# Moving layer 2's mask from the scores to the sigmoids, on GpSimd, in a four-layer graph network with new instruction orders

## The chip, the cores and the metric

One NeuronCore of one Trainium2 chip runs the whole program. The metric is the device time of one execution in microseconds (us). The engines are TensorE (PE, with its weight loads as PEld), VectorE (DVE), ScalarE (ACT), GpSimd (POOL) and SyncE (SP), which issues nearly all the transfers. Each engine runs its own list of instructions in order; they meet only at semaphores.

## What is computed

Thirty-two graphs of 256 nodes with 128 features each go through four layers. Each adds its result to its input and normalises the sum:

```
x = layernorm(x + L0(x, adj))   # graph attention: softmax over neighbours of leaky(s_i + d_j), times h
x = layernorm(x + L1(x, adj))   # the same with other weights
x = layernorm(x + L2(x, adj))   # sigmoid(leaky((x*a0) @ x.T)) where adj == 1, and 0 where adj == 0; times x
x = layernorm(x + L3(x, adj))   # sum over neighbours, times a 128x128 weight, plus bias
```

Only layer 2 matters here. `adj` holds 0 and 1. An entry with `adj == 0` must have weight 0, and an entry with `adj == 1` has weight sigmoid(leaky(score)), where leaky(s) is the larger of s and 0.2 s. Since sigmoid rises everywhere, this is the larger of sigmoid(s) and sigmoid(0.2 s).

## The kernel before

The graphs go through in 16 teams of two (`H = 2`); a step named `score:5` does its work for both graphs of team 5. Every engine has a string of such steps in the table `ORDER` (written out by hand or by a tool, and fixed), and the program emits the instructions in exactly that order. There is no scheduler at run time: an engine whose next step waits for a semaphore stands still, with everything behind it. `BANKS` gives the PSUM bank (of 8) for every product of every team; PE waits for the last reader of a bank before it writes there. Rings of buffers in SBUF (`RAW`, `MASK`, `SG`, `WGT`, `XB` and so on teams deep) set how far apart the teams may be.

What happens to one team, with the engine that does it before the change:

- PE projects (`h0`), DVE takes the two attention logits (`logits0`), PE and DVE find their maximum (`dT0`, `peak0`, `top0`, `dmax0`), DVE subtracts it (`shift0`), ACT takes exponentials (`gains0`) and scales the values (`vals0`). PE spreads a row (`rows0`), DVE makes the masked weights (`weight0`, four instructions of 128x256), PE multiplies them with the values (`out0`), DVE divides by the row sums and adds the input (`rsum0`, `rinv0`, `res0`), and takes the statistics (`stats0`, `var0`). POOL raises the variance to the power -1/2 (`pow0`). Layer 1 repeats this with `1` in the names; `center1` and `norm1` end it.
- Layer 2: PE transposes (`xT2`), ACT copies with a factor (`xTa`), PE forms the scores (`score`). In the same accumulation PE adds a second product for each block: the tile `raw`, which is 1 - adj, times `minus_big`, -1e30 on the diagonal. A score without an edge so becomes -1e30, and both sigmoids of it are 0. ACT takes sigmoid(s) into `sg` and sigmoid(0.2 s) into `wgt` (step `sigmoid`), DVE writes the larger into `wgt` (step `alpha`), and PE multiplies (`out2`). DVE adds `xb`, which is x plus bias from POOL (`bias2`), and takes statistics (`res2`, `stats2`, `var2`); `pow2` is on POOL, and `norm2` on ACT or DVE.
- Layer 3: the normalised x is split into two half-precision parts (`high` on ACT, `low` on POOL), PE gathers over the mask (`agg`), ACT copies, PE multiplies (`out3`), DVE does `res3`, `stats3`, `var3`, POOL `pow3`, ACT or DVE `norm3`; SP stores.

From each adjacency tile (int32) two 16-bit tiles are made: `raw` by DVE (`make_raw`) and the mask `maskT` by ACT (`make_mask`). DVE also ORs each team's `raw` into `seen` (`note_seen`), and `judge` tests at the end whether any entry was other than 0 or 1; then a general path would run, which never happens for these inputs.

The lines that the prediction names are L731 `make_raw`, L738 `note_seen`, L754 and L538 the biases on DVE and POOL, L765 `norm` on DVE, L791 `shift`, L797 `fscale`, L815 `alpha`, L841 `res2` and `res3`, L856 statistics, L862 to L869 the variances, L873 `center1`, L542 the powers and L547 `low` on POOL, L571 `make_mask` and L637 `norm1` on ACT, L1089 and L1090 the two products of a score.

## Time and profile before

| what | value |
|---|---|
| device time, three runs | 270.17, 268.92, 270.03 us; median 270.03 |
| profiled execution, first to last instruction (span) | 268.6 us |
| instructions | 6069 |
| DVE busy | 247.2 us (92%) |
| PE busy | 237.0 us (88%) |
| ACT busy | 217.9 us (81%) |
| POOL busy | 139.0 us (52%) |
| DMA, share of 16 engines' span | under 24% in all queues |
| granted TensorE clock, mean | 0.978 of full |

The profile gives its execution's span and no other time of its own: 268.6 us lies 1.4 us under the median of the timed runs. "Busy" is time in which at least one instruction of the engine is open; a short instruction on DVE overlaps its follower by some 0.07 us, so a group's busy time is a little under its count times its mean. PE's busy time counts the latency of each product and not only its pitch.

### The profile page before, as it was taken

To read this page: it belongs to the slowest core of one execution; us is meant where nothing else is said; L and a number is where in the kernel's file an instruction comes from. 1 tells how busy PE (TensorE), PEld (TensorE's weight loads), DVE (VectorE), ACT (ScalarE), POOL (GpSimd) and SP (SyncE) were. 2 spreads that over 40 slices of the span, in tenths; PEclk is the share of its full clock that TensorE was granted. 3 is DMA by queue.
4 is the path that set the end of the run, shared out by engine and by line. 5 is a ranking of instruction groups with operands and counts; after the bars stand their busy time and mean duration, and the time that the engine had idled before them with its cause. 6 is when DMAs were issued, how large, how long until landed. Compare 5 with 4: busy or idle time off the path is not lost.

```text
span 268.6 us, 6069 instructions
## 1 busy us (share of the span) xinstructions
PE 237.0 (88%) x1825; PEld 210.1 (78%) x1825; DVE 247.2 (92%) x956; ACT 217.9 (81%) x626; POOL 139.0 (52%) x161
## 2 busy tenths in 40 slices
PE   7887969889998999999999899999999959996850
PEld 7765768678886989888898788988999859785740
DVE  1598998999999989999999999999999999999883
ACT  1366525688899999899899999999999979977841
POOL 1001102511384485689647717554598457778851
PEclk9999988999999999999999999999999999999985
DMA  6597371000070003506000633103000110100033
GB/s 237 193 307 264 118 248 67 1 2 0 2 263 13 2 0 115 202 14 221 1 5 0 198 114 122 41 1 121 0 2 0 41 41 7 36 0 1 4 117 122
DMA packets 12147, 21.79 MB, mean 81 GB/s; under 512 B 1104, under 2 KB 5968, under 8 KB 12112
## 3 DMA queue, kind: packets, MB, share of 16 engines
q1 hardware_dynamic: 11680, 21.17, 22.9%
q8 instruction: 16, 0.26, 0.4%
q10 hardware_dynamic: 432, 0.20, 0.3%
q14 instruction: 19, 0.16, 0.2%
HBM read 17.17 MB, written 4.19 MB: 80 GB/s over the span
## 4 chain that ended last, share of the span: by engine, by line
DVE 49%; PE 28%; issue 8%; POOL 6%; ACT 5%; DMA 2%; DVEq 0%; POOLq 0%; ACTq 0%
PE banks L1123 13%; DVE wgt_all L808 10%; DVE fstats L856 8%; DVE fres L849 7%; DVE fres L841 5%; POOL frstd L542 4%; DVE wgt_all L815 3%; PE banks L1089 3%; DVE raw_all L731 3%; PE banks L1064 2%; PE banks L1120 2%; PE banks L1133 2%; DMA adj_all<-adj_turned 2%; PE banks L1081 1%; PE banks L1049 1%
## 5 line engine op out<-in xcount | busy, mean ns | idle before, releaser
L542 POOL TENSOR_TENSOR frstd<-fvar,minus_half 128x4 f32<-128x4 f32 x64 | 74.2, 1165 | 104.7 <-DVE fvar L862 36.6
L1123 PE MATMUL banks<-vals_all,wgt_all 128*128 128x129 f32 x512 | 64.4, 279 | 3.1 <-DVE wgt_all L808 2.9
L1123 PEld LDWEIGHTS banks<-vals_all,wgt_all 128*128 128x128 f32 x512 | 60.6, 194 | 4.8 <-issue 3.2
L808 DVE SCALAR_TENSOR_TENSOR wgt_all<-banks,gain,maskT 128x256 f32<-128x256 f32 x128 | 52.6, 473 | 0.6 <-PE banks L1081 0.3
L538 POOL TENSOR_TENSOR xb<-xs_all,bias_cen 128x256 f32<-128x256 f32 x60 | 44.1, 760 | 8.6 <-DVE xs_all L765 4.4
L856 DVE BATCH_NORM_STATS2 fstats<-fres 128x6 f32<-128x256 f32 x128 | 47.8, 416 | 0.0
L1089 PE MATMUL banks<-fxT,fxTa 128*128 128x256 f32 x128 | 35.8, 382 | 0.0
L1123 PE MATMUL banks<-xs_all,wgt_all 128*128 128x128 f32 x256 | 31.6, 277 | 4.8 <-DVE wgt_all L815 4.7
L1123 PEld LDWEIGHTS banks<-xs_all,wgt_all 128*128 128x128 f32 x256 | 29.9, 192 | 5.4 <-issue 3.2
L640 ACT ACTIVATE xs_all<-fres,frstd 128x128 f32<-128x128 f32 x96 | 30.9, 425 | 1.9 <-POOL frstd L542 1.8
L578 ACT COPY fxT<-banks 128x256 f32<-128x256 f32 x64 | 21.1, 396 | 10.9 <-PE banks L1049 10.8
L637 ACT ACTIVATE xs_all<-fres,fcenter,frstd 128x128 f32<-128x128 f32 x64 | 26.6, 500 | 3.7 <-DVE fcenter L873 3.7
L547 POOL TENSOR_TENSOR fxTa<-xs_all,fxTa 128x256 f16<-128x256 f32 x30 | 21.2, 728 | 11.0 <-ACT fxTa L620 11.0
L841 DVE TENSOR_TENSOR fres<-banks,xb 128x256 f32<-128x256 f32 x64 | 23.8, 414 | 2.0 <-PE banks L1123 1.2
L1089 PEld LDWEIGHTS banks<-fxT,fxTa 128*128 128x128 f32 x128 | 19.3, 191 | 5.8
L815 DVE TENSOR_TENSOR wgt_all<-sg_all,wgt_all 128x512 f32<-128x512 f32 x32 | 22.2, 728 | 1.0 <-ACT wgt_all L614 1.0
L1081 PE MATMUL banks<-ident,gain 128*128 128x128 f32 x128 | 19.1, 277 | 3.7 <-ACT vals_all L586 3.4
L613 ACT ACTIVATE sg_all<-banks 128x512 f32<-128x512 f32 x32 | 19.3, 602 | 3.4 <-PE banks L1090 3.3
L595 ACT ACTIVATE vals_all<-banks,fscale 128x128 f32<-128x128 f32 x64 | 18.4, 393 | 2.9 <-DVE fscale L797 2.9
L1064 PE MATMUL banks<-w_fast,fxT 128*128 128x130 f32 x128 | 17.9, 282 | 2.1 <-DVE fres L849 1.4
L1120 PE MATMUL banks<-w_cen,fxT 128*128 128x128 f32 x128 | 17.9, 284 | 1.8 <-ACT fxT L625 1.5
L585 ACT ACTIVATE gain<-shift 128x8 f32<-128x8 f32 x32 | 6.8, 211 | 15.5 <-DVE shift L791 15.2
(95 smaller groups left out, 463.1 us busy)
## 6 DMA issues: line engine op xcount, KB each, us to landing
adj_all<-adj_turned SPq DMA_DIRECT2D x16, 512.0 KB, 4.8
xT_all<-x_turned SPq DMA_DIRECT2D x16, 256.0 KB, 4.7
x_all<-x_laid SPq DMA_DIRECT2D x16, 256.0 KB, 4.4
out<-xs_all SPq DMA_DIRECT2D x16, 256.0 KB, 2.4
bias<-biases_laid SPq DMA_DIRECT2D x1, 128.0 KB, 3.6
w_pack<-W_and_columns ACTq DMA_DIRECT2D x1, 68.0 KB, 2.6
w_fast<-W_turned ACTq DMA_DIRECT2D x1, 64.0 KB, 4.1
w_nat<-in_L_gnn_W ACTq DMA_DIRECT2D x1, 64.0 KB, 4.4
```

The costliest lines, as they stand in the source:

```text
L538: nc.gpsimd.tensor_tensor(xb(u)[:, :, :], xs(u)[:, :, :], bias_cen[:, int(l) - 2, :, :], ALU.add).then_inc(fast_pool[k], 1)
L542: nc.gpsimd.tensor_tensor(frstd[:, int(l), slot(n), :], fvar[:, int(l), slot(n), :], minus_half[:, :, :], ALU.pow).then_inc(fast_pool[k], 1)
L637: last = nc.scalar.activation(xs(u)[:, b, :], fres(u)[:, b, :], ACT.Identity, bias=fcenter[:, u, b:b + 1], scale=frstd[:, 1, u, b:b + 1])
L640: last = nc.scalar.activation(xs(u)[:, b, :], fres(u)[:, b, :], ACT.Copy, scale=frstd[:, int(l), u, b:b + 1])
L808: last = nc.vector.scalar_tensor_tensor(out=wgt(u)[:, c, :], in0=place(f"rows{l}", u), scalar=gain[:, u, c, 1:2], in1=maskT(u)[:, c, :], o ...
L815: nc.vector.tensor_tensor(wgt(u), sg(u), wgt(u), ALU.max).then_inc(fast_dve[k], 1)
L841: nc.vector.tensor_tensor(fres(u)[:, :, :], place(f"out{l}", u).rearrange("p (b c) -> p b c", b=NB), xb(u)[:, :, :], ALU.add).then_inc(fas ...
L856: nc.vector.bn_stats(fstats[:, u, :, :].rearrange("p b k -> p (b k)"), fres(u)[:, :, :].rearrange("p b d -> p d b")).then_inc(fast_dve[k], 1)
L1064: last = nc.tensor.matmul(place(f"h{l}", u)[:, b * HC:(b + 1) * HC], (xT_in if l == "0" else fxT)(u)[:, b * P:(b + 1) * P], w_fast[:, int( ...
L1089: nc.tensor.matmul(place("score", u)[:, c * N:(c + 1) * N], fxTa(u)[:, c * P:(c + 1) * P], fxT(u)[:, :], start=True, stop=False)
L1120: last = nc.tensor.matmul(place("out3", u)[:, b * D:(b + 1) * D], fxT(u)[:, b * P:(b + 1) * P], w3_cen[:, :], start=True, stop=True)
L1123: last = nc.tensor.matmul(place(f"out{l}", u)[:, b * width:(b + 1) * width], wgt(u)[:, c, b * P:(b + 1) * P], (vals if l in "01" else xs)( ...
```

## The change

1. `raw`, `minus_big` and the 64 products of L1090 are gone. Scores hold no mask.
2. DVE takes the larger sigmoid into `sg` (`larger`, step `umax`, 32 instructions as before, only the output differs). A new POOL step `alpha` multiplies it with the mask into `wgt`: 32 instructions of 128x512, float32 times bfloat16. `out2` now waits for POOL.
3. `seen` reads the mask instead of `raw`, still on DVE; `adj` buffers are free once the mask is made.
4. Steps have new doers. The masks of teams 0, 12, 14 and 15 are made by DVE, the others by ACT. `norm1` of teams 4 and 15 goes from ACT to DVE. The `res3` of teams 0 to 5 becomes an ACT copy out of PSUM (`lift3`) and a POOL addition. Of 64 small variance steps 17 go to POOL. DVE has 5 bias teams instead of 2, 3 `low` instead of 1, one `high` instead of none, and 4 `norm2` instead of 5 (`norm3` stays at 3); POOL keeps 27 bias teams and 13 `low`.
5. All five orders and all banks are new; rings: `ADJ` 4 for 3, `MASK` 10 for 9, `SG` 4 for 3, no `RAW`.

```diff
-X_IN, XT_IN, ADJ, RAW, MASK, XS, FXT, FXTA, VALS, WGT, SG, FRES, XB = 4, 3, 3, 7, 9, 6, 7, 5, 6, 7, 3, 9, 5
+X_IN, XT_IN, ADJ, MASK, XS, FXT, FXTA, VALS, WGT, SG, FRES, XB = 4, 3, 4, 10, 6, 7, 5, 6, 7, 4, 9, 5
...
     "sp": (
-        "xT:0 adj:0 xT:1 xT:2 adj:2 adj:1 x:0 adj:3 xT:3 x:3 xT:4 adj:4 adj:6 x:2 xT:7 x:1 adj:5 adj:9 x:5 x:6 adj:8 "
+        "xT:0 xT:1 x:0 adj:0 x:2 xT:2 adj:1 adj:2 x:1 x:3 xT:3 adj:3 xT:4 adj:4 xT:5 adj:5 x:4 adj:6 xT:6 x:5 adj:7 "
...
     "pool": (
-        "low:13 pow3:11 pow2:15 pow3:12 low:15 pow2:14 bias3:15 pow3:13 pow3:15 pow3:14"
+        "pow2:11 var3:10 pow3:10 bias3:11 low:11 pow1:14 pow1:15 alpha:12 pow3:11 bias2:14 alpha:13 pow2:12 alpha:14 "
+        "alpha:15 pow2:13 pow2:14 bias3:13 pow2:15 low:14 low:15 bias3:15 pow3:12 pow3:13 var3:14 pow3:14 pow3:15"
...
+            def residual(l, n, k):
+                for u in graphs(n):
+                    biaser = doer(f"bias{l}", n)
+                    pool.wait_ge(signals[biaser][k], at(biaser, f"bias{l}", u))
+                    pool.wait_ge(fast_act[k], at("act", f"lift{l}", u))
+                    nc.gpsimd.tensor_tensor(fres(u)[:, :, :], fres(u)[:, :, :], xb(u)[:, :, :], ALU.add).then_inc(fast_pool[k], 1)
...
+                nc.gpsimd.tensor_scalar(var, squares, factor, floor, ALU.mult, ALU.add).then_inc(fast_pool[k], 1)
...
+            def alpha(l, n, k):
+                for u in graphs(n):
+                    pool.wait_ge(fast_dve[k], at("dve", "umax", u))
+                    nc.gpsimd.tensor_tensor(wgt(u), sg(u), maskT(u), ALU.mult).then_inc(fast_pool[k], 1)
...
             def sigmoids(l, n, k):
                 if n >= SG:
-                    act.wait_ge(fast_dve[(n - SG) % K], at("dve", "alpha", final(n - SG)))
+                    act.wait_ge(fast_pool[(n - SG) % K], at("pool", "alpha", final(n - SG)))
...
+            def lift(l, n, k):
+                act.wait_ge(fast_pe[k], at("pe", f"out{l}", final(n)))
+                for u in graphs(n):
+                    nc.scalar.copy(fres(u)[:, :, :], place(f"out{l}", u).rearrange("p (b c) -> p b c", b=NB)).then_inc(fast_act[k], 1)
...
-            def make_raw(l, n, k):
-                for u in graphs(n):
-                    dve.wait_ge(fast_adj_in[u // H % ADJ], loaded(u, ADJ))
-                    if n >= RAW:
-                        dve.wait_ge(fast_pe[(n - RAW) % K], at("pe", "score", u - RAW * H))
-                    nc.vector.tensor_scalar(raw(u), adj_in(u)[:, :, :], -1.0, 1.0, ALU.mult, ALU.add).then_inc(fast_dve[k], 1)
...
+            def larger(l, n, k):
+                for u in graphs(n):
+                    dve.wait_ge(fast_act[k], at("act", "sigmoid", u))
+                    nc.vector.tensor_tensor(sg(u), sg(u), wgt(u), ALU.max).then_inc(fast_dve[k], 1)
...
-            def alpha(l, n, k):
-                for u in graphs(n):
-                    dve.wait_ge(fast_act[k], at("act", "sigmoid", u))
-                    nc.vector.tensor_tensor(wgt(u), sg(u), wgt(u), ALU.max).then_inc(fast_dve[k], 1)
...
                     for c in range(NB):
-                        nc.tensor.matmul(place("score", u)[:, c * N:(c + 1) * N], fxTa(u)[:, c * P:(c + 1) * P], fxT(u)[:, :], start=True, stop=False)
-                        last = nc.tensor.matmul(place("score", u)[:, c * N:(c + 1) * N], minus_big[:, :], raw(u)[:, c, :], start=False, stop=True)
+                        last = nc.tensor.matmul(place("score", u)[:, c * N:(c + 1) * N], fxTa(u)[:, c * P:(c + 1) * P], fxT(u)[:, :], start=True, stop=True)
...
                     elif l == "2":
-                        pe.wait_ge(fast_dve[k], at("dve", "alpha", u))
+                        pe.wait_ge(fast_pool[k], at("pool", "alpha", u))
```

The orders are read here as instructions, at the places that the prediction speaks of. First DVE at the program's start, from the first logits on. Before:

```order
L775 COPY logit<-banks 128x4 x2
L783 TENSOR_REDUCE top<-banks 4x1
L731 TENSOR_SCALAR raw_all<-adj_all 128x512 x2
L787 TENSOR_REDUCE dmax<-banks 128x2
L791 TENSOR_TENSOR shift<-logit,dmax 128x8
L695 BN_STATS mean_stats<-w_nat 128x6
L697 MEMSET wait_carrier 128x1
L698 BN_AGGR mean_mv<-mean_stats 128x2
L700 TENSOR_SCALAR w_cen<-w_nat,mean_mv 128x128
L738 TENSOR_TENSOR seen<-seen,raw_all 128x512
```

The same place with the change (L766 is the mask made by DVE):

```order
L817 COPY logit<-banks 128x4 x4
L825 TENSOR_REDUCE top<-banks 4x1 x2
L829 TENSOR_REDUCE dmax<-banks 128x2
L833 TENSOR_TENSOR shift<-logit,dmax 128x8
L723 BN_STATS mean_stats<-w_nat 128x6
L725 MEMSET wait_carrier 128x1
L726 BN_AGGR mean_mv<-mean_stats 128x2
L728 TENSOR_SCALAR w_cen<-w_nat,mean_mv 128x128
L829 TENSOR_REDUCE dmax<-banks 128x2
L833 TENSOR_TENSOR shift<-logit,dmax 128x8
L766 CAST mask_all<-adj_all 128x512 x2
```

The two `raw` and the `seen` instructions between the small ones of team 0 are gone from there; the logits of teams 0 and 1 stand together, and the first mask is made by DVE just ahead of the first weights.

POOL about the middle of the program, around the biases and powers of teams 6 to 10. Before:

```order
L538 TENSOR_TENSOR xb<-xs_all,bias_cen 128x256 x4
L542 TENSOR_TENSOR frstd<-fvar,minus_half 128x4 x2
L538 TENSOR_TENSOR xb<-xs_all,bias_cen 128x256 x2
L542 TENSOR_TENSOR frstd<-fvar,minus_half 128x4 x4
L547 TENSOR_TENSOR fxTa<-xs_all,fxTa 128x256 x2
L542 TENSOR_TENSOR frstd<-fvar,minus_half 128x4 x2
```

With the change (L535 bias, L540 power, L546 `low`, L553 the addition of `res3`, L559 variance, L569 the new `alpha`):

```order
L546 TENSOR_TENSOR fxTa<-xs_all,fxTa 128x256 x2
L535 TENSOR_TENSOR xb<-xs_all,bias_cen 128x256 x2
L559 TENSOR_SCALAR fvar<-fstats 128x4
L540 TENSOR_TENSOR frstd<-fvar,minus_half 128x4
L553 TENSOR_TENSOR fres<-fres,xb 128x256 x2
L559 TENSOR_SCALAR fvar<-fstats 128x4
L540 TENSOR_TENSOR frstd<-fvar,minus_half 128x4
L569 TENSOR_TENSOR wgt_all<-sg_all,mask_all 128x512 x2
L540 TENSOR_TENSOR frstd<-fvar,minus_half 128x4
L569 TENSOR_TENSOR wgt_all<-sg_all,mask_all 128x512 x2
L540 TENSOR_TENSOR frstd<-fvar,minus_half 128x4 x2
```

The long multiplications stand between the powers, so a power behind them waits for them.

POOL at the end. Before, the last rows are:

```order
L538 TENSOR_TENSOR xb<-xs_all,bias_cen 128x256 x2
L547 TENSOR_TENSOR fxTa<-xs_all,fxTa 128x256 x2
L542 TENSOR_TENSOR frstd<-fvar,minus_half 128x4 x3
L547 TENSOR_TENSOR fxTa<-xs_all,fxTa 128x256 x2
L542 TENSOR_TENSOR frstd<-fvar,minus_half 128x4
L538 TENSOR_TENSOR xb<-xs_all,bias_cen 128x256 x2
L542 TENSOR_TENSOR frstd<-fvar,minus_half 128x4 x3
```

With the change, from `alpha` of team 12 on:

```order
L569 TENSOR_TENSOR wgt_all<-sg_all,mask_all 128x512 x2
L540 TENSOR_TENSOR frstd<-fvar,minus_half 128x4
L535 TENSOR_TENSOR xb<-xs_all,bias_cen 128x256 x2
L569 TENSOR_TENSOR wgt_all<-sg_all,mask_all 128x512 x2
L540 TENSOR_TENSOR frstd<-fvar,minus_half 128x4
L569 TENSOR_TENSOR wgt_all<-sg_all,mask_all 128x512 x4
L540 TENSOR_TENSOR frstd<-fvar,minus_half 128x4 x2
L535 TENSOR_TENSOR xb<-xs_all,bias_cen 128x256 x2
L540 TENSOR_TENSOR frstd<-fvar,minus_half 128x4
L546 TENSOR_TENSOR fxTa<-xs_all,fxTa 128x256 x4
L535 TENSOR_TENSOR xb<-xs_all,bias_cen 128x256 x2
```

Eight multiplications now stand in the last stretch of POOL, four of them in a row (teams 14 and 15). Team 15 is the last of every engine, and teams 12 to 15 go through layers 2 and 3 side by side. Behind the last `umax` DVE still has 4 teams of `res3` and `stats3`, 3 of `res2` and `stats2`, and 2 of bias, 2 of `low`, one `high` and one `norm2`.

## Rows read from the trace of the kernel before

**Rows 1.** The page: span, and busy time, share and instructions of each engine.

```profile
span 268.6 us, 6069 instructions
...
PE 237.0 (88%) x1825; PEld 210.1 (78%) x1825; DVE 247.2 (92%) x956; ACT 217.9 (81%) x626; POOL 139.0 (52%) x161
```

**Rows 2.** Stretches of the span: length, busy us of each engine, clock, DMA.

```profile
core 0: us, PE busy (x) PEld busy (x) DVE busy (x) ACT busy (x) POOL busy (x), PEclk, DMA share, GB/s
0.00:15.00 15.00, 11.77 (x74) 10.97 (x75) 6.62 (x30) 5.48 (x13) 0.74 (x7) 1.00 0.62 225
15.00:70.00 55.00, 46.76 (x350) 40.83 (x350) 52.88 (x234) 34.47 (x109) 12.21 (x13) 0.97 0.34 114
...
150.00:213.00 63.00, 62.30 (x509) 57.27 (x508) 61.43 (x251) 61.96 (x180) 37.53 (x45) 1.00 0.19 64
...
252.00:269.00 17.00, 6.48 (x48) 5.09 (x46) 10.57 (x35) 7.51 (x24) 7.38 (x9) 0.74 0.28 95
```

**Rows 3.** PE in time order, one score's products: start, us, count.

```profile
193.50 0.27 PE L1090 MATMUL banks<-raw_all,minus_big 128*128 128x256 bf16 x1
193.61 0.60 PE L1089 MATMUL banks<-fxT,fxTa 128*128 128x256 f32 x2
```

**Rows 4.** Groups by line and form: busy us, mean ns, idle before them.

```profile
L542 POOL TENSOR_TENSOR frstd<-fvar,minus_half 128x4 f32<-128x4 f32 x64 | 74.2, 1165 | 104.7 <-DVE fvar L862 36.6 <-DVE fvar L864 31.9 <-DVE fvar L867 19.5
...
L538 POOL TENSOR_TENSOR xb<-xs_all,bias_cen 128x256 f32<-128x256 f32 x60 | 44.1, 760 | 8.6 <-DVE xs_all L765 4.4 <-ACT xs_all L640 3.1 <-ACT xs_all L637 1.1
...
L815 DVE TENSOR_TENSOR wgt_all<-sg_all,wgt_all 128x512 f32<-128x512 f32 x32 | 22.2, 728 | 1.0 <-ACT wgt_all L614 1.0
L547 POOL TENSOR_TENSOR fxTa<-xs_all,fxTa 128x256 f16<-128x256 f32 x30 | 21.2, 728 | 11.0 <-ACT fxTa L620 11.0
...
L731 DVE TENSOR_SCALAR raw_all<-adj_all 128x512 bf16<-128x512 int32 x32 | 12.4, 427 | 1.0 <-DMA adj_all<-adj_turned 1.0
...
L765 DVE TENSOR_SCALAR xs_all<-fres,frstd 128x128 f32<-128x128 f32 x32 | 7.7, 303 | 1.1 <-POOL frstd L542 1.1
...
L862 DVE TENSOR_SCALAR fvar<-fstats 128x4 f32<-128x4 f32 x16 | 3.0, 187 | 0.0
...
L754 DVE TENSOR_TENSOR xb<-xs_all,bias_cen 128x256 f32<-128x256 f32 x4 | 1.5, 418 | 0.0
```

**Rows 5.** The same view, small DVE forms and `res2`/`res3`.

```profile
L841 DVE TENSOR_TENSOR fres<-banks,xb 128x256 f32<-128x256 f32 x64 | 23.8, 414 | 2.0 <-PE banks L1123 1.2 <-PE banks L1120 0.8
...
L791 DVE TENSOR_TENSOR shift<-logit,dmax 128x8 f32<-128x8 f32 x32 | 7.2, 231 | 0.1
...
L873 DVE SCALAR_TENSOR_TENSOR fcenter<-fstats,frstd 128x4 f32<-128x4 f32 x16 | 4.9, 308 | 1.2 <-POOL frstd L542 1.2
...
L777 DVE TENSOR_TENSOR logit<-banks,frstd 128x4 f32<-128x4 f32 x32 | 3.5, 150 | 0.4 <-POOL frstd L542 0.4
```

**Rows 6.** POOL and DVE in time order: start us, us, instruction.

```profile
94.35 1.03 POOL L542 TENSOR_TENSOR frstd<-fvar,minus_half 128x4 f32<-128x4 f32 x1
...
96.59 2.80 POOL L542 TENSOR_TENSOR frstd<-fvar,minus_half 128x4 f32<-128x4 f32 x1 [1.22 <-ACT fxT L625]
...
96.65 0.67 DVE L738 TENSOR_TENSOR seen<-seen,raw_all 128x512 int32<-128x512 int32 x1
...
97.25 1.27 DVE L815 TENSOR_TENSOR wgt_all<-sg_all,wgt_all 128x512 f32<-128x512 f32 x2
...
99.37 1.42 POOL L538 TENSOR_TENSOR xb<-xs_all,bias_cen 128x256 f32<-128x256 f32 x2
99.43 0.68 DVE L873 SCALAR_TENSOR_TENSOR fcenter<-fstats,frstd 128x4 f32<-128x4 f32 x1 [0.91 <-POOL frstd L542]
```

**Rows 7.** Line L815: count, shortest, median and longest ns.

```profile
L815 DVE TENSOR_TENSOR wgt_all<-sg_all,wgt_all x32: 670/680/1222, 70.6 to 250.7; 128x512 f32<-128x512 f32 x32
```

**Rows 8.** DVE in time order, at the start and the last `alpha`.

```profile
9.76 0.74 DVE L731 TENSOR_SCALAR raw_all<-adj_all 128x512 bf16<-128x512 int32 x2
...
250.73 0.69 DVE L815 TENSOR_TENSOR wgt_all<-sg_all,wgt_all 128x512 f32<-128x512 f32 x1 [0.33 <-ACT wgt_all L614]
```

More of the change, by code:

```diff
@@ L461, in loaded @@
             return u // (depth * H) * 16 + 16
+        SEEN = [n for name, l, n in order("dve") if name == "seen"]
+        VARIANCE = {"0": (EPS / D, EPS * EPS), "2": (1 / (D * UP_SQUARE), EPS / UP_SQUARE), "3": (1 / D, EPS * UP_SQUARE)}
         signals = {"pe": fast_pe, "act": fast_act, "dve": fast_dve, "pool": fast_pool}
@@ L643, in _ @@
             steps = {"mask": make_mask, "xT": copy_xT, "gains": gains, "vals": values, "xTa": copy_xTa, "sigmoid": sigmoids,
-                     "high": high_part, "agg": copy_gathered, "norm": normalize}
+                     "high": high_part, "agg": copy_gathered, "norm": normalize, "lift": lift}
             for step, l, n in order("act"):
@@ L893, in judge @@
                 nc.vector.tensor_reduce(bad[:, 8:9], bad[:, 3:7], AX.X, ALU.max).then_inc(bad_step, 1)
-            steps = {"raw": make_raw, "mask": make_mask, "bias": biases, "low": low_part, "norm": normalize, "seen": note_seen, "fscale": scales, "logits": logits, "peak": peak, "dmax": largest, "shift": shifts,
-                     "weight": weights, "rsum": row_sums, "rinv": inverses, "alpha": alpha, "res": residual,
+            steps = {"mask": make_mask, "high": high_part, "umax": larger, "bias": biases, "low": low_part, "norm": normalize, "seen": note_seen, "fscale": scales, "logits": logits, "peak": peak, "dmax": largest, "shift": shifts,
+                     "weight": weights, "rsum": row_sums, "rinv": inverses, "res": residual,
                      "stats": statistics, "var": variances, "center": centers}
@@ L1144, in _ @@
             for n in range(TEAMS - K, TEAMS):
-                pe.wait_ge(fast_dve[n % K], at("dve", "res3", final(n)))
+                signal, engine, step = emptied_by("out3", n)
+                pe.wait_ge(signal[n % K], at(engine, step, final(n)))
             pe.wait_ge(bad_step, 3)
```

98 lines of the change are left out of this document (63 added, 35 removed), and 193 rows, old and new, of tables (BANKS, ORDER).

## The prediction

> **What bounds the kernel now.** I read the page's busy line first [rows 1]: DVE is busy 247.2 of 268.6 us, PE 237.0, ACT 217.9, POOL 139.0. The table by stretch [rows 2] says where the rest lies. DVE stands still for 8.4 us of the first 15 and for 6.4 of the last 17; in the 237 us between it is idle 7 us in all. PE is full only from 150 to 213 us (62.3 of 63), and there DVE is busy 61.4 too. So DVE sets the pace nearly everywhere, with PE beside it in one stretch, and what counts is DVE's busy time, idle time that cannot be filled at either end, and what makes DVE's instructions longer. POOL did 126.1 us of its work after 70 us (139.04 less 0.74 and 12.21), 63% of that time.
>
> The third view is the order in time about 97 us [rows 6], and it decides this forecast. A power on POOL takes 1.03 us when nothing disturbs it. The one issued at 96.59 takes 2.80: in its first 1.9 us DVE runs `seen` and two `alpha`, each of which reads two tiles of SBUF. At 99.37 it is the other way round: POOL starts two bias additions of 0.7 us, and DVE's `center1`, a four-element instruction begun 0.06 us later, takes 0.68 us, until the first addition is over. Long POOL instructions and DVE instructions that read SBUF twice shut each other out. How often: `shift` averages 231 ns and `center1` 308 [rows 5], where L777, as small but with one input from PSUM, averages 150; that is 32 x 0.08 + 16 x 0.16 = 5.1 us. `alpha` averages 728 against a shortest of 670 [rows 4, 7], 1.9 us; the variance L862 averages 187 against 150, 0.6 us. So at least 7.6 us of DVE's 247 are waits inside instructions, which no idle figure shows. On POOL the powers hold 74.2 - 64 x 1.03 = 8.3 us of the same kind [rows 4, 6].
>
> The Trainium skill ("SBUF — State Buffer", Who interferes with whom) states this as an exclusive lock on a port pair: a DVE instruction with two SBUF inputs, or in a two-port mode, and a GpSimd instruction that reads SBUF exclude each other for a whole instruction. The trace agrees with 2.80 against 1.03 us.
>
> **The change part by part.** One instruction's price is its group's busy time over its count [rows 4, 5].
>
> DVE work. `raw` goes: -12.4 us. Four teams of masks come, 8 instructions as long as `raw`'s 0.39: +3.1. Two teams of `norm1` come and one of `norm2` goes, net 4 at 0.24 (L765): +1.0. Three bias teams come, 6 at 0.38 (L754): +2.3; two `low` and one `high` team, 6 taken at the same 0.38: +2.3. Six `res3` teams leave, 12 at 0.37 (L841): -4.5. Seventeen variances leave at 0.19: -3.2. `umax` costs what `alpha` did, `seen` what it did. Sum: -11.4 us.
>
> PE. 64 products of L1090 go. The next product starts 0.11 us behind such a one [rows 3], so -7.0 us of pitch. PE is the limit only in 150 to 213, a quarter of the run, and DVE has 1.6 us of slack there, so I count -1 of them; bounds 0 and -2.
>
> ACT loses four mask teams and two `norm1` teams and gains six `lift3` and one `norm2`; it is the limit nowhere, and I count nothing. If DVE got much faster ACT's 217.9 would be next, far off.
>
> POOL. No row shows 512 elements or a bfloat16 input on POOL. From below: a bias addition of 256 elements, 0.70 us; from above two of them with the mean of 0.76, 1.5 us. I take 1.4, two at the undisturbed pitch of rows 6 (1.42 for two), since the long part is per element. 32 x 1.4 = +44.8. Six bias and four `low` instructions leave (-4.4 and -2.8), 12 additions of `res3` come (+8.8), 17 variances: between DVE's 0.19 and a power's 1.03, taken at 0.3, +5. POOL rises from 139 to about 190. The first `alpha` was at 70.6 us [rows 7], so nearly all of this falls behind 70 us: about 176 us there, 89% of what was 198.6.
>
> The Trainium skill ("GPSIMD Engine Reference", Elementwise) gives about 2.6 cycles an element for two inputs; 256 elements more would make `alpha` an estimated 1.25 us and POOL 5 us lighter. Its table of engine selection advises against such work on GpSimd.
>
> The port. A POOL instruction of length L catches a DVE instruction that comes at a random time for L x L / 2 on average. Before there were 90 long ones of 0.7: 90 x 0.49 = 44. Now there are 92 of them and 32 of 1.4: 45 + 63 = 108, 2.45 times as much. DVE's exposed instructions are about a tenth fewer, since `raw` is gone and normalisations and additions come. So 7.6 us become about 17: +9. Bounds: 0 if the multiplications fall beside instructions that read PSUM (`weight`, `res0`, statistics have one SBUF input at most), and +22 if each holds DVE for half its length (32 x 0.7).
>
> The start. Before, `raw` was made in gaps of the first teams' chain of tiny steps, the first at 9.76 us [rows 8], where DVE idles for 8.4 us anyway. Work that only filled gaps saves nothing when removed. The first four teams' `raw` are 2.8 us; I give back 2 (0 to 2.8). The adjacency of team 0 is loaded fourth instead of second, but the mask is a single step ahead of the first weights; no charge.
>
> The tail. `out2` used to start right behind `alpha`. Now POOL's 1.4 us a graph lies between, and the last stretch of POOL has eight such instructions, with powers and a bias in the same queue, while DVE's `umax`, bias, `norm` and `low` there read SBUF twice. Behind the last `umax` DVE still has 15 us of work: 10 instructions of bias, `low` and `high` at 0.38, 4 of `norm2` at 0.24, 14 of `res` at 0.37 and 14 of statistics, taken at the same 0.37. That is more than the 10.6 us it is busy in the last 17 now [rows 2], and it hides part of the latency. Bounds: +1.4 (one multiplication bare) and +11.2 (all eight). I take +3, nearer to the low end because of that work. What is late next is `pow2` of team 15, then its `low`, `agg` and the last store.
>
> Sum: -11.4 - 1 + 9 + 2 + 3 = +1.6. The span becomes 270.2. The profiled execution lies 1.4 us under the median of its three timed runs, so I forecast 271.6 us against 270.03.
>
> **The rivals.** *The saving arrives* (0.27). The port costs less than I say because the new order keeps multiplications away from exposed instructions. For it speaks that DVE is plainly the limit and loses 11 us of plain work, against it the density of exposed instructions: nearly every team has shifts, a centre, a scale and a `seen`. With +2 at the port, +1 at the start and +1.4 at the tail: -11.4 - 1 + 4.4 = -8, 262 us. It decides once the port's growth stays under some 5 us.
>
> *POOL becomes the bound* (0.23). It has 176 us to do after 70 us, more with its own waits for the port (8.3 us on the powers before, perhaps 18 now): 186. It runs in order, and a power behind two multiplications is 2.8 us late; DVE's `center1`, ACT's `norm` and the next layer wait for it. If POOL idles only 8% of the rest through waits of its own, it ends at 70 + 186/0.92 = 272, and the last normalisation and store follow, 5 us: 277 span, 278 us. For it speaks the 89%, against it that POOL has stood idle for 104.7 us waiting for variances and can be late without harm as long as the rings are deep. It decides where POOL passes some 93% of the time from 70 us on.
>
> *The forecast itself* (0.50): the saving is given back through the port and at both ends, 268 to 276, centre 271.6.
>
> **How the numbers follow.** A measurement of this kernel can tell about 0.5%, 1.35 us: faster is under 268.7, slower over 271.4. Of the forecast's 0.50 I give 0.12 to faster, 0.18 to the same and 0.20 to slower, its centre being at the upper edge; of the first rival's 0.27 it is 0.25 faster and 0.02 the same; the second is slower throughout. Together 0.37, 0.20, 0.43. The range must reach into both rivals: down to 261, up to 280, with a tenth left out on either side.
>
> **What would show it.** DVE busy near 245 to 248 although its instructions sum to 11 us less; mean of `shift` and `center1` above 300 ns, and of `umax` above 728; `alpha` on POOL near 1.4 us and POOL at 185 to 200 us busy; PE busy down by about 17 us, since each L1090 is open for 0.27; DVE idle in the first 15 us over 9 us; POOL released by DVE in the last 20 us less often than DVE or PE by POOL. I am wrong on the port if the small forms keep their means, wrong on the price if `alpha` is far from 1.4, and wrong on the middle if DVE, between 15 us and the tail, idles much more than the 7 us of now: then a new wait in the order, not the port, would be the cause.

## The result

The changed kernel takes 288.01 us (median of 4 runs, 286.86 to 289.61) beside 270.1 us of the kernel before on the same chip (268.92 to 272.77, 4 runs). The ratio is 1.067, its 95% interval 1.059 to 1.075: slower by some 18 us. The forecast was 271.6 us, the range 261 to 280. The profiled execution took 289.61 us for a span of 287.7. Here and below, executions in which a kernel ran some us longer at a lower granted clock are left out of the ratios; that leaves e7 with two, 267.3 and 267.7 us, and without a ratio.

The page after, span and busy time (before in [rows 1]):

```profile
span 287.7 us, 5917 instructions
...
PE 239.4 (83%) x1761; PEld 214.1 (74%) x1761; DVE 255.8 (89%) x918; ACT 212.7 (74%) x622; POOL 182.4 (63%) x212
```

38 DVE instructions fewer, and DVE is busy 8.6 us longer. Stretches of the changed kernel, columns as in [rows 2]:

```profile
0.00:15.00 15.00, 11.28 (x67) 10.34 (x68) 6.17 (x29) 5.11 (x15) 0.73 (x7) 0.93 0.89 317
...
15.00:70.00 55.00, 45.42 (x339) 39.69 (x338) 51.94 (x205) 36.37 (x106) 19.48 (x22) 0.99 0.44 146
...
150.00:213.00 63.00, 57.75 (x444) 52.77 (x443) 57.84 (x213) 54.13 (x163) 49.23 (x57) 0.97 0.10 31
...
252.00:288.00 36.00, 19.16 (x134) 16.98 (x132) 25.97 (x67) 18.75 (x56) 25.99 (x26) 0.83 0.12 38
```

Between 150 and 213 us, where PE and DVE both were full, neither is now: PE 57.8 and DVE 57.8 of 63. The last stretch is the second thing to see. From the same start at 252 us it is 36 us long where it was 17, and DVE works 26 us of it.

Groups of DVE after (line, operation, tiles, count, busy us, mean ns, idle before; the old ones are in [rows 4, 5]):

```profile
L808 DVE TENSOR_TENSOR sg_all<-sg_all,wgt_all 128x512 f32<-128x512 f32 x32 | 23.6, 774 | 0.8 <-ACT wgt_all L638 0.8
...
L758 DVE TENSOR_TENSOR seen<-seen,mask_all 128x512 int32<-128x512 int32 x16 | 12.1, 756 | 0.1
L833 DVE TENSOR_TENSOR shift<-logit,dmax 128x8 f32<-128x8 f32 x32 | 11.3, 354 | 0.1
L904 DVE TENSOR_SCALAR fvar<-fstats 128x4 f32<-128x4 f32 x31 | 8.6, 278 | 0.3
...
L908 DVE SCALAR_TENSOR_TENSOR fcenter<-fstats,frstd 128x4 f32<-128x4 f32 x16 | 6.4, 401 | 0.3 <-POOL frstd L540 0.3
L776 DVE TENSOR_TENSOR xb<-xs_all,bias_cen 128x256 f32<-128x256 f32 x10 | 5.2, 554 | 0.0
...
L766 DVE CAST mask_all<-adj_all 128x512 bf16<-128x512 int32 x8 | 4.0, 534 | 0.0
L819 DVE TENSOR_TENSOR logit<-banks,frstd 128x4 f32<-128x4 f32 x32 | 3.5, 150 | 0.5 <-PE banks L1106 0.3
```

`shift` rose from 231 to 354 ns and `center1` from 308 to 401, while L819, as small but with one input from PSUM, still averages 150. What they wait for stands in the order in time. DVE after, about 98 us:

```profile
98.54 0.27 DVE L825 TENSOR_REDUCE top<-banks 4x1 f32<-4x128 f32 x1
98.74 3.02 DVE L808 TENSOR_TENSOR sg_all<-sg_all,wgt_all 128x512 f32<-128x512 f32 x2
101.68 0.15 DVE L829 TENSOR_REDUCE dmax<-banks 128x2 f32<-128x4 f32 x1
101.75 0.21 DVE L861 SCALAR_TENSOR_TENSOR fsum<-banks,frstd 128x2 f32<-128x2 f32 x2
101.88 0.91 DVE L833 TENSOR_TENSOR shift<-logit,dmax 128x8 f32<-128x8 f32 x1
```

POOL at the same time:

```profile
98.10 5.78 POOL L569 TENSOR_TENSOR wgt_all<-sg_all,mask_all 128x512 f32<-128x512 f32 x4 [0.38 <-DVE sg_all L808]
```

Two maxima that take 1.29 us elsewhere take 3.02 under POOL's multiplications, and a `shift` 0.91.

To put one number on this I take, for each form of DVE instruction, what its durations lie above the form's lower quartile, counting those over it by more than 15% and 20 ns. These "waits inside" sum to 10.5 us before and 25.4 after. So DVE's busy time rose by 8.6: the waits grew by 14.9, and the plain work fell by only 6.3. DVE's idle time rose by 10.5, from 21.4 to 31.9.

A second cut needs only the end of the last maximum (`alpha` before, `umax` after) and the span. Before, it ends at 251.4 [rows 8] with 17.1 us to go. After:

```profile
259.33 1.28 DVE L808 TENSOR_TENSOR sg_all<-sg_all,wgt_all 128x512 f32<-128x512 f32 x2
```

That is 260.6, with 27.1 to go: 9.2 us later, and then a tail 10.0 longer. Nearly all experiments below are read by these figures.

### The profile page after: what moved, and what is told of

Its sections match the earlier page's. It is cut to its first block, busy times and chain, and to the rows that moved or that the text cites. A ratio compares the mean times of both kernels' runs of the same rounds, so it can differ in the third digit from the quotient of the medians.

```text
span 287.7 us, 5917 instructions
## 1 busy us (share of the span) xinstructions
PE 239.4 (83%) x1761; PEld 214.1 (74%) x1761; DVE 255.8 (89%) x918; ACT 212.7 (74%) x622; POOL 182.4 (63%) x212
## 4 chain that ended last, share of the span: by engine, by line
DVE 49%; PE 30%; ACT 8%; issue 7%; POOL 4%; DVEq 0%; ACTq 0%; POOLq 0%
PE banks L1164 15%; DVE wgt_all L850 9%; DVE fstats L894 7%; DVE fres L886 6%; DVE sg_all L808 5%; PE banks L1106 4%; PE banks L1131 4%; DVE fres L878 3%; PE banks L1091 2%; DVE shift L833 2%; ACT xs_all L669 2%; PE banks L1123 2%; DVE seen L758 2%; PE banks L1174 2%; DVE xs_all L802 2%
## 5 line engine op out<-in xcount | busy, mean ns | idle before, releaser
L540 POOL TENSOR_TENSOR frstd<-fvar,minus_half 128x4 f32<-128x4 f32 x64 | 67.0, 1051 | 18.9 <-DVE fvar L900 10.1
L850 DVE SCALAR_TENSOR_TENSOR wgt_all<-banks,gain,mask_all 128x256 f32<-128x256 f32 x128 | 52.5, 474 | 1.7 <-PE banks L1123 1.5
L535 POOL TENSOR_TENSOR xb<-xs_all,bias_cen 128x256 f32<-128x256 f32 x54 | 40.0, 759 | 19.7 <-ACT xs_all L666 17.4
L569 POOL TENSOR_TENSOR wgt_all<-sg_all,mask_all 128x512 f32<-128x512 f32 x32 | 43.7, 1389 | 7.5 <-DVE sg_all L808 7.5
L1164 PE MATMUL banks<-xs_all,wgt_all 128*128 128x128 f32 x256 | 36.4, 303 | 6.0 <-POOL wgt_all L569 3.7
L669 ACT ACTIVATE xs_all<-fres,frstd 128x128 f32<-128x128 f32 x100 | 31.9, 410 | 8.7 <-POOL frstd L540 8.7
L559 POOL TENSOR_SCALAR fvar<-fstats 128x4 f32<-128x4 f32 x17 | 4.5, 264 | 47.7 <-DVE fstats L894 47.7
L1131 PE MATMUL banks<-fxT,fxTa 128*128 128x256 f32 x128 | 31.0, 385 | 1.3 <-DVE fres L886 0.5
L808 DVE TENSOR_TENSOR sg_all<-sg_all,wgt_all 128x512 f32<-128x512 f32 x32 | 23.6, 774 | 0.8 <-ACT wgt_all L638 0.8
L878 DVE TENSOR_TENSOR fres<-banks,xb 128x256 f32<-128x256 f32 x52 | 19.4, 412 | 4.8 <-PE banks L1164 4.7
L637 ACT ACTIVATE sg_all<-banks 128x512 f32<-128x512 f32 x32 | 19.6, 613 | 1.4 <-PE banks L1131 1.2
L1123 PEld LDWEIGHTS banks<-ident,gain 128*128 128x128 f32 x128 | 15.3, 145 | 6.2 <-DVE wgt_all L850 5.0
L638 ACT ACTIVATE wgt_all<-banks 128x512 f32<-128x512 f32 x32 | 19.8, 619 | 0.0
```

The source lines that it names most:

```text
L535: nc.gpsimd.tensor_tensor(xb(u)[:, :, :], xs(u)[:, :, :], bias_cen[:, int(l) - 2, :, :], ALU.add).then_inc(fast_pool[k], 1)
L540: nc.gpsimd.tensor_tensor(frstd[:, int(l), slot(n), :], fvar[:, int(l), slot(n), :], minus_half[:, :, :], ALU.pow).then_inc(fast_pool[k], 1)
L569: nc.gpsimd.tensor_tensor(wgt(u), sg(u), maskT(u), ALU.mult).then_inc(fast_pool[k], 1)
L669: last = nc.scalar.activation(xs(u)[:, b, :], fres(u)[:, b, :], ACT.Copy, scale=frstd[:, int(l), u, b:b + 1])
L808: nc.vector.tensor_tensor(sg(u), sg(u), wgt(u), ALU.max).then_inc(fast_dve[k], 1)
L850: last = nc.vector.scalar_tensor_tensor(out=wgt(u)[:, c, :], in0=place(f"rows{l}", u), scalar=gain[:, u, c, 1:2], in1=maskT(u)[:, c, :], o ...
```

## The experiments

Each ran beside the kernel before on one chip, in five groups, whose medians of before are 270.37 (e1 to e4), 270.90 (e5 to e8), 272.46 (e9 to e12), 271.87 (e13 to e16) and 271.10 us (e17, e18). Ratios are to these, with 95% intervals. The span, waits inside and tail are from each kernel's profiled execution. e1, e2, e7, e8, e10, e12, e15, e16 and e17 leave out part of what is computed, e14 most of the test of the entries; they are there for their times alone.

| kernel | us | ratio | span | DVE busy | waits inside | last maximum | tail |
|---|---|---|---|---|---|---|---|
| before | 270.1 | 1 | 268.6 | 247.2 | 10.5 | 251.4 | 17.1 |
| after | 288.0 | 1.067 | 287.7 | 255.8 | 25.4 | 260.6 | 27.1 |
| e1 alpha of 4 numbers | 272.0 | 1.007 (1.004 to 1.011) | 270.4 | 239.1 | 8.1 | 245.6 | 24.7 |
| e2 alpha as a power | 271.2 | 1.006 (1.002 to 1.011) | 269.2 | 239.4 | 8.3 | 244.6 | 24.6 |
| e3 old orders, new mask | 296.8 | 1.102 (1.091 to 1.113) | 293.3 | 255.4 | 27.8 | 272.7 | 20.7 |
| e4 old orders, lifted | 271.6 | 1.005 (1.000 to 1.010) | 268.3 | 237.0 | 8.7 | 251.0 | 17.2 |
| e5 new orders, lifted | 278.1 | 1.024 (1.014 to 1.034) | 276.5 | 241.4 | 9.3 | 250.5 | 26.0 |
| e6 alpha in halves | 287.5 | 1.061 (1.051 to 1.070) | 284.7 | 253.9 | 23.4 | 259.4 | 25.4 |
| e7 old orders, bare | 269.6 | none | 265.9 | 236.8 | 9.1 | 246.7 | 19.2 |
| e8 e3 as a power | 286.8 | 1.059 (1.051 to 1.067) | 284.9 | 238.0 | 9.3 | 264.2 | 20.6 |
| e9 alpha on DVE | 292.0 | 1.075 (1.063 to 1.086) | 289.7 | 259.5 | 10.0 | 263.2 | 26.4 |
| e12 one input | 282.8 | 1.043 (1.033 to 1.052) | 279.7 | 246.7 | 17.0 | 253.4 | 26.3 |
| e13 `seen` twice | 280.8 | 1.033 (1.021 to 1.044) | 278.9 | 258.1 | 11.0 | 262.4 | 16.5 |
| e14 `seen` small | 263.7 | 0.974 (0.965 to 0.982) | 261.6 | 239.2 | 9.7 | 244.4 | 17.2 |
| e16 no read | 273.0 | 1.006 (1.002 to 1.010) | 271.3 | 240.9 | 11.6 | 245.6 | 25.7 |

### GpSimd's reads, or its step

e1 and e2 keep the changed kernel whole, orders too, and change one line each.

```diff
-nc.gpsimd.tensor_tensor(wgt(u), sg(u), maskT(u), ALU.mult)
+nc.gpsimd.tensor_tensor(wgt(u)[:, 0, 0:4], sg(u)[:, 0, 0:4], maskT(u)[:, 0, 0:4], ALU.mult)      # e1
+nc.gpsimd.tensor_tensor(idle_pow[:, u, :, :], minus_half[:, :, :], minus_half[:, :, :], ALU.pow)  # e2
```

> The changed kernel, but POOL's alpha multiplies 4 elements instead of 512, behind the same waits; so the sigmoids go unmasked into out2. Port theory: DVE's waits inside instructions fall back (shift's mean from 354 ns to about 230, center1's from 401 to about 300), DVE busy from 256 to about 241, time 270 to 274 us. Order theory (the new orders are bad by themselves): DVE busy falls as well, but its idle time grows by as much and the time stays above 282 us. POOL-latency theory (the 1.15 us of each multiplication in the queue is what is late): time also falls to about 272, so this run separates these two only from the order theory; the next one separates them.

> As the run before, but each multiplication is replaced by a power of 4 elements into a scratch tile, behind the same waits: it keeps POOL for 1.0 us, nearly as long as the 1.15 us of the multiplication, and reads almost nothing from SBUF; the sigmoids go unmasked into out2. Port theory: as fast as the run with 4 elements within 2 us, 271 to 276 us, with shift's mean near 230 ns. POOL-latency theory: as slow as the changed kernel, 284 to 288 us. Order theory: also 282 or more, with DVE busy near 241.

272.0 and 271.2 us. e2 settles more, since its step lasts 1.0 us as before and POOL stays busy 174 us; the page of e2:

```profile
span 269.2 us, 5917 instructions
...
PE 232.1 (86%) x1761; PEld 209.3 (78%) x1761; DVE 239.4 (89%) x918; ACT 211.4 (79%) x622; POOL 174.2 (65%) x212
```

With the step and its place kept and the two long reads gone, 18.5 of the span's 19.1 us of loss are gone, 16.4 of them in DVE's busy time and 2.1 in its idle time. Both runs also leave out the long write; e16 below keeps it. A step of 1.0 us on POOL (e2) costs no more than one of 0.38 (e1), so neither POOL's occupancy nor the latency of its step costs anything that can be seen in the new orders. And the rest of the change, the 8 us less of DVE's busy time included, is worth nothing: 1.006 of before. The table says how: against before, the last maximum comes 6.8 us earlier and the tail is 7.5 longer.

### The same work on DVE instead

e9 does the multiplication on DVE, right behind each `umax`, and not on POOL.

```diff
+                    nc.vector.tensor_tensor(wgt(u), sg(u), maskT(u), ALU.mult).then_inc(fast_dve[k], 1)
```

> The changed kernel with the multiplication by the mask done by DVE, right behind each maximum, and none on GpSimd: 32 instructions of 128x512 more on DVE, 21 to 22 us at the 0.68 us of a maximum, and no reads by GpSimd that shut it out. Port theory (GpSimd's 44.5 us of multiplications cost DVE some 15 to 17 us of waits inside its instructions, nearly as much as doing the work itself): 288 to 293 us, waits inside DVE's instructions back to some 9 us, DVE busy about 261. Latency theory (what costs is the GpSimd step between maximum and product, and powers queued behind it): 275 to 282 us.

292.0 us: 32 instructions of 0.69 us, and the waits inside are back at 10.0. This is the price list of the offload. On DVE the multiplication is 22 us of work; on POOL it makes DVE wait 17 us more than in e2. 44.5 us of GpSimd work spared DVE 3.7 us of busy time and the kernel 2.0 us of span. The intervals of the two ratios overlap (1.063 to 1.086, and 1.059 to 1.075), so the runs don't show that doing it on DVE is slower.

### How the waits depend on the instruction

e6 cuts each multiplication in two, e12 gives it one input, e16 none (`nc.gpsimd.memset(wgt(u), 0.5)`).

```diff
+                    for c in range(NB):                                                        # e6
+                        last = nc.gpsimd.tensor_tensor(wgt(u)[:, c, :], sg(u)[:, c, :], maskT(u)[:, c, :], ALU.mult)
+                    nc.gpsimd.tensor_scalar(wgt(u), sg(u), 1.0, None, ALU.mult)                # e12
```

> The changed kernel, each GpSimd multiplication of 512 elements a row cut into two of 256 (64 instead of 32). If a held port catches DVE for what is left of one GpSimd instruction (waits go with the square of its length), the 15 us of added waits inside DVE's instructions fall by about half: 278 to 283 us, DVE busy 248 to 250. If GpSimd keeps the port through instructions that follow each other, or if the order and not the waits costs the time: 286 to 292 us, DVE busy 254 to 258.

> The changed kernel, GpSimd's step multiplying the maximum by the constant 1 instead of by the mask: one input from SBUF instead of two, the mask left out. If only a GpSimd instruction with two inputs shuts DVE out: DVE's waits inside instructions fall to about 9 us and the time to 270 to 274. If any read of SBUF by GpSimd does, for as long as the instruction lasts: with the instruction no shorter, 284 to 288 us; if it takes half the time (about 0.6 us), some 277 to 281.

> The changed kernel, GpSimd's step filling the weights with the constant 0.5 instead of multiplying (maximum and mask both left out): 128x512 float32 written and nothing read. If reads shut DVE out: waits inside DVE's instructions about 8 us, 268 to 272 us. If any long access to SBUF by GpSimd does: waits of 12 us or more, 275 us or more.

e6 came out in the range of its second theory: 287.5 us, waits 23.4, of which 15.1 are growth over e2 where the whole multiplication has 17.1. It doesn't settle the law, though. By the shortest times measured (two pieces of 0.66 us for one of 1.15) a law with the square of the length asks for 11.3, one with the plain time for 19.6, and 15.1 lies between. What settles more is how long each instruction waited. In the changed kernel 21 DVE instructions waited under a multiplication, for 0.8 us on average, and 17 of them for 0.75 to 1.0 us; in halves 35 did, for 0.4 us on average, and 26 of them for 0.40 to 0.51. An instruction that came at a random time would wait for anything between nothing and the whole length. These wait for most of a multiplication, so they come soon after it began. No wait in e6 is longer than one piece, so the port isn't kept through pieces that follow each other, as the second theory had it. In the rows about 98 us the two engines take turns: each `umax` waits for the multiplication that began before it, and the next multiplication for that `umax`. Whether most of the 21 came about in this way was not counted.

The one-input step of e12 (median 1.49 us, longer than the multiplication's 1.25) added 8.7 us of waits over e2 and not 17, in more POOL time; 282.8 us lies between the two theories, so here an instruction with one input disturbs about half as much. About as many DVE instructions waited under it, but none for more than 0.45 of its 1.48 us. e16's fill takes 0.52 us a time; the waits are 11.6 and the time that of e2 within the intervals. The Trainium skill ("SBUF — State Buffer", Who interferes with whom) says that a DVE instruction with two SBUF inputs contends with a GpSimd instruction that reads SBUF, not with one that only writes it. e16 agrees: its waits are 3.3 us over e2's, and no DVE instruction with two such inputs waited under a fill. Five others did, for 2.7 us in all: two variances, two normalisations and a mask.

### Orders and mask method apart

e3 puts the new mask method under the orders, banks and doers of before, with POOL's `alpha` queued where DVE's ended in the trace of before; e8 is e3 with the power of e2. e4 and e5 keep the mask in the scores without `raw`: PE adds 256 x mask, and the sigmoids take it off by their bias; e4 under the old orders, e5 under the new. e7 is e4 without any of it (bare: no `raw`, no second product, no bias, unmasked).

```diff
-last = nc.tensor.matmul(..., minus_big[:, :], raw(u)[:, c, :], start=False, stop=True)
+last = nc.tensor.matmul(..., plus_lift[:, :], maskT(u)[:, c, :], start=False, stop=True)    # e4, e5
-nc.scalar.activation(sg(u), scored, ACT.Sigmoid)
+nc.scalar.activation(sg(u), scored, ACT.Sigmoid, bias=floors[:, 0:1])                       # e4, e5
```

> The new way of masking under the old orders, banks and doers: no raw, umax on DVE, the multiplication on POOL put where DVE's alpha ended in the trace of before; seen moves behind weight0. Port theory alone: DVE loses 12 us of raw and gains about 15 of port waits, 270 to 275 us. Order theory: the new orders are what costs, so this is 262 to 269 us. POOL-latency theory: 275 to 285 us, since the old orders leave no time between alpha and out2.

> Old orders, and neither raw nor a multiplication on POOL: PE adds 256 times the mask itself to the scores, and ACT takes 256 off again as the bias of both sigmoids, so that entries without an edge come out as 0. DVE writes the larger sigmoid into wgt as before the change. If raw's 12 us of DVE work are worth what they take, 258 to 263 us; if the removed work only filled gaps or PE is the second bound at once, 264 to 268 us. All theories agree that it is faster than before; if it is not, DVE's busy time is the wrong measure.

> The new orders, banks and doers, with the mask kept inside the scores: TensorE adds 256 times the mask, both sigmoids take it off again through their bias, DVE writes the larger one straight to the weights, and GpSimd multiplies nothing. With the old orders under this mask (already measured: 271.58 us, with no `raw` left) it makes four corners: two orders, two places of the mask. Balance theory (the kernel before is held by DVE, TensorE and ScalarE together, and the new orders gain some 7 us in the middle and lose as many behind the last maximum): 267 to 272 us. DVE theory (DVE's busy time alone sets the pace, the old orders kept the saving from arriving): 258 to 264 us, DVE idle under 22 us.

> The orders, banks and doers of the kernel before, with the mask work of layer 2 left out: no `raw`, no second product in the scores, no mask bias, no multiplication on GpSimd (the sigmoids are left unmasked). It prices what the change removes, alone. DVE theory: DVE loses 12 us of 247, 258 to 261 us. Balance theory: `raw` filled gaps at the start, and ScalarE, busy 39.7 of 40 us between 70 and 110 us, and TensorE stay as they were, so most of it falls away: 264 to 268 us.

> The kernel of e3 (new mask method, orders of before), its GpSimd multiplication replaced by a power of 8 numbers a row into a scratch tile, as long in time (1.0 us) but with no long read of SBUF; DVE's maximum lands in `sg`, and the sigmoids stay unmasked. Port theory: what made e3 296.8 us is the same thing that made the changed kernel 288, 270 to 275 us. Placement theory (the old orders have no room for one more step between maximum and product, and GpSimd's powers stand behind it): 284 to 292 us.

e3 and e8 refute the theory that the reads are the whole matter under any order (us, the groups' chips differ):

| | no POOL step behind the maximum | POOL step, no long reads | POOL step with reads |
|---|---|---|---|
| old orders | 269.6 (e7, unmasked) | 286.8 (e8) | 296.8 (e3) |
| new orders | not run | 271.2 (e2) | 288.0 (after) |

Under the old orders the bare step costs 17 us (19 of span), with `out2` waiting (PE behind POOL's step 15.0 us in e8) and DVE idle for 47 us, 18 more than in e7. The new orders make that step nearly free, as e1 and e2 show. That is what they buy, and the tail shows what they pay: old orders end 16.5 to 20.7 us behind the last maximum in every run, new orders 24.6 to 27.1, whatever the mask method.

e4 and e7 missed what I expected of them (258 to 263, and 258 to 261 or 264 to 268): DVE loses 10 us of busy time and the kernel gains 1 us or nothing. e5 at 278.1 missed too: with 64 products more than e2, a bias in each sigmoid and no step on POOL it is 7 us slower, 5.3 of its 7.3 us of span idle time of DVE, for which I have no test. With the mask in the scores the new orders are thus 6.5 us slower than the old (e4), with no step and no long reads of layer 2 on POOL.

### Why the freed DVE time was worth nothing

e10 and e11 are e7 and e4 with the masks of teams 9 to 15 moved from ACT to DVE, where `raw` was (mask ring of 12).

> The kernel of e7 (orders of before, mask work of layer 2 left out, sigmoids unmasked), with the adjacency masks of teams 9 to 15 made by DVE where it used to make `raw`, instead of by ScalarE, and a mask ring 12 teams deep. DVE gets 5.5 us of work back, ScalarE loses 9. Balance theory (the 10 us taken from DVE were lost because ScalarE and TensorE held the pace, ScalarE above all between 70 and 110 us): 261 to 266 us. DVE theory: 272 to 275 us, e7 plus what DVE gets. Third theory (the written order itself holds the time, no engine's sum): 267 to 271 us.

> The kernel of e4 (orders of before, mask kept in the scores as plus 256, taken off by the sigmoids' bias, no `raw`), computing everything, with the same move of seven teams of masks to DVE and the ring of 12. ScalarE pays 6 us for the bias of 64 sigmoids (0.70 against 0.60 us) and gets 9 back. Balance theory: 264 to 268 us, under the kernel before. Order theory: 270 to 273 us, as e4.

274.2 us (1.007, 1.003 to 1.011) and 273.1 us (1.006, 1.001 to 1.011): the theory that ScalarE held the pace found nothing. e10 lies where its DVE theory put it: DVE got 5.2 us of busy time more than in e7 and the span grew by 6.3, on another chip and at a mean clock of 0.969 for 0.988. e11, with the same move, has the ratio of e4. So I changed the load of one engine of the kernel before, orders untouched: `seen` twice (e13), `seen` on 8 values (e14), the second sigmoid on 4 (e15).

```diff
+                for again in (1, 2):                                                           # e13, seen itself as before
+nc.vector.tensor_tensor(seen[:, :, 0, 0:4], seen[:, :, 0, 0:4], raw_all[:, pair(n, RAW), 0, 0:8].bitcast(I32), ...)  # e14
+nc.scalar.activation(wgt(u)[:, 0, 0:4], place("score", u)[:, 0:4], ACT.Sigmoid, scale=SLOPE)   # e15
```

> The kernel before, with DVE's step `seen` (an OR of two tiles, 16 instructions of 0.75 us) done twice for each team: 12 us more DVE work, everything else as it was. DVE theory (the sum of DVE's work is the pace, both ways): 280 to 283 us. Kink theory (no slack for more work on DVE, but others as full, so that less work gives nothing back): 279 to 283 us as well; what tells them apart is e14. Slack theory (the written order holds the pace and DVE has room in it): under 275 us.

> The kernel before, with `seen` cut to 8 values a row and team (the test for other entries than 0 and 1 is left nearly out): 9 to 10 us less DVE work, and DVE's longest reads of two tiles gone. DVE theory: 260 to 262 us. Kink theory: 267 to 270 us, DVE idle 28 to 31 us instead of 21.

> The kernel before, with ScalarE's second sigmoid cut to 4 numbers a row (the sigmoid of 0.2 times the score is left out elsewhere, so the weights are wrong): 12 to 13 us less ScalarE work of 218. ScalarE theory (it was the hidden bound where DVE's saving stopped): 262 to 266 us. Order theory or DVE theory: 268 to 271 us.

10.9 us more of DVE cost 10.3 of span (8.8 by the ratio), 8.0 less gave back 7.0 (7.2 by the ratio), and 12.4 less on ACT gave nothing (270.7 us, 1.002, 0.998 to 1.007). DVE is the bound, both ways, as the prediction read it, if `seen` stands for all of its work; it is the only step that was both added and taken away. e14 missed both ranges, on the side of DVE. It is also the cleanest mirror of e2: the same 239 us of DVE, the same last maximum (244.4 and 244.6), and 7.4 us between their tails, which are 7.6 us of span.

Then how could e7 give so little? e17 is e14 with `raw` of teams 7 to 15 cut small in place; e18 is e4 with `seen` back in its old place for 11 teams.

> The kernel of e14 (orders of before, `seen` nearly left out), with `raw` of teams 7 to 15 cut to 4 numbers a block as well, so that later scores use stale tiles: 18 instructions at 0.39 us shrink to about 0.1, 5 us less DVE work behind 70 us, nothing moved. If `raw` is DVE work like any other: 258 to 260 us where e14 had 263.7. If it only fills gaps while others hold the pace: 262 to 264 us.

> The kernel of e4, which computes everything (mask in the scores as plus 256, no `raw`, 12 us less DVE work), with `seen` back at its place in the order of before for 11 of 16 teams (teams 9 to 12 and 14 stay behind their first weights, as their masks come too late) and a mask ring of 12. If the moved step ate the gain of e4 and e7: 263 to 267 us. If `raw` is worth little in itself, or the whole written order leans on it: 269 to 272 us, as e4.

e17: 264.5 us (ratio 0.973, 0.964 to 0.982), just above both of its ranges and the same as e14, with 3.8 us less on DVE. From 190 to 230 us the granted clock was 0.91 in its profile and 1.00 in e14's, so a stretch at full clock is read, 70 to 110 us (up to 190 us, from 40 on, PE had done 1177 matmuls in e17 and 1173 in e14, no more in spite of the lighter DVE). First e17, columns as in [rows 2]:

```profile
70.00:110.00 40.00, 39.27 (x311) 35.07 (x310) 38.07 (x150) 39.65 (x116) 24.52 (x29) 1.00 0.32 100
```

and the same stretch of before, where DVE had 38.51, PE 37.86 and ACT 38.11:

```profile
70.00:110.00 40.00, 37.86 (x292) 33.02 (x291) 38.51 (x130) 38.11 (x108) 23.08 (x24) 1.00 0.25 86
```

I read this as a floor some 7 us under the kernel before: there PE (98%) and ACT (99%) are full as well, and DVE's further microseconds become idle ones. It rests on e17 alone, and a rival fits as well: that `raw`'s time is worth nothing in itself, while `seen`'s is. e4 and e7, which drop `raw` and keep `seen`, gained 1 us or nothing too; cutting `raw` alone in the kernel before was not run. e7, at 265.9 of span, lies above the floor, so the floor doesn't explain it. e18 (271.6 us, 1.005, 0.997 to 1.014) did not bring the gain back, so the moved `seen` was not what ate it. Which wait keeps e4 and e7 from 262 stays open; those kernels differ from before in more places of DVE's order than I could undo one by one.

No version tried that computes everything beats the kernel before.

## Why the prediction was wrong

**The bound was read rightly.** e13 to e15 price DVE's microsecond at 0.8 to 0.9 in both directions and ACT's at nothing.

**The step that failed first: the port's +9.** "A POOL instruction of length L catches a DVE instruction that comes at a random time for L x L / 2." With this I scaled up the 7.6 us of waits read from before. The waits inside grew by 14.9 us over before, 17.1 over e2, and not by 9. The length was not at fault: at the measured 1.15 us the same scaling gives some 6, an estimate from the same rows. The random time was: most of the DVE instructions that were caught waited 0.75 to 1.0 us, nearly a whole multiplication. So DVE stands for about 0.4 us per us in which POOL reads two tiles (17.1 of 44.5). My upper bound of +22 held it; that bound, half a length for each of 32, is 18.4 at 1.15 us, and 17.1 is close under it.

**The second: the tail's +3.** It is +10.0. I counted "15 us of work" behind the last `umax`, set it against 10.6 us before, and then let it hide a latency, where it had itself to be added. Behind the last maximum DVE is busy for 17.4 us after, 15.8 in e2 and 11.2 before, and idle for 9.7, 8.8 and 5.9: 6.2 of the 10.0 are work and waits inside it, 3.8 idle time. 7.5 of the 10 stay when POOL's reads are gone (e2), 2.5 come from them. What is late at the very end I named rightly in kind (`pow2`, `norm3`, store) but not in size: teams 12 to 15 go side by side, so the last normalisations fall together. ACT at the end, first before:

```profile
261.74 1.28 ACT L640 ACTIVATE xs_all<-fres,frstd 128x128 f32<-128x128 f32 x4 [0.76 <-POOL frstd L542]
```

and after:

```profile
266.40 1.28 ACT L669 ACTIVATE xs_all<-fres,frstd 128x128 f32<-128x128 f32 x4 [6.63 <-POOL frstd L540]
...
276.85 4.78 ACT L669 ACTIVATE xs_all<-fres,frstd 128x128 f32<-128x128 f32 x16 [1.03 <-POOL frstd L540]
```

ACT waits 6.63 us for `pow2` behind four `alpha` in a row (POOL's row at 258.22 lasts 7.19), and later writes four teams at once, whose stores then leave together: 6.1 us from the last normalisation to the end, 3.6 before.

**The work term, -11.4, was -6.3** by busy time less waits inside. The groups of e2, nearly free of new waits, say where it was mis-sized: `raw` (-12.4) and `res3` (-4.4) fell and the masks (+3.0) came as counted, but the variances saved 1.8 instead of 3.2, `norm` cost 1.9 instead of 1.0 (a `norm1`, which takes a centre too, lasts 0.39 us and not 0.30), the biases 2.7 instead of 2.3, and `seen` 0.8 instead of nothing. Its whole busy time fell by 7.8. In the changed kernel masks and biases wait as well: 534 and 554 ns each, 414 and 461 in e2.

**The start, +2:** idle time of DVE up to 40 us went from 9.7 to 11.8. Right. **PE's -1** can't be seen; PE's busy time did not fall by 17 but rose by 2.4. In e2 it fell by 4.9; the mean granted clock was 0.978 before, 0.974 in e2 and 0.955 after, and what share of the difference is the clock's was not separated. I also called ACT far off as the next bound; if the floor is read rightly, ACT and PE stand 7 us away.

**Sum.** Predicted +1.6 of span, measured +19.1. The 17.5 between them: waits inside 5.9 more than said, plain work 5.1 less saved, and idle time of 10.5 instead of the +4 of start, tail and PE together, 6.5.

**The price of `alpha`** came out right by luck: mean 1.389 us, but 1.15 at its shortest, and I read the rest as its own waits for DVE.

```profile
L569 POOL TENSOR_TENSOR wgt_all<-sg_all,mask_all x32: 1149/1251/3412, 59.7 to 264.1; 128x512 f32<-128x512 f32 x32
```

(That row, by tile, gives shortest, median and longest.) The Trainium skill's figure ("GPSIMD Engine Reference", Elementwise), from which I estimated 1.25, agrees better than the 1.4 that I took. POOL is busy 182 and not 190.

**Signs that I named.** `shift` and `center1` over 300 ns and the maximum over 728: seen (354, 401, 774). DVE busy 245 to 248: 255.8. DVE idle over 9 in the first 15: 8.8, much as before. DVE idle in the middle: 9.9 us from 40 to 230 against 4.8, a small new wait beside the port: e2, without the reads, has 8.7, so it belongs to the orders, and I can't name one cause of it. In the last 20 us POOL waits for DVE once, and DVE and PE for POOL twice; before it was five times and twice. That sign came true.

**The rivals.** *POOL becomes the bound* gave the nearest time, 278, for a reason that did not happen: behind 70 us POOL is busy 162 of 218 us, 75% and not 93, and e1 and e2 show its occupancy to cost nothing that can be seen. That the time lies near its range is luck. *The saving arrives* is refuted by after, and even without the reads (e2) only as far as the last maximum.
